# Adding the output bias of an attention block to the constant bin of its spectrum instead of to the whole of x

## The reference

```python
q = (layernorm(x) @ Wq + bq);  k = (ctx @ Wk + bk);  v = (ctx @ Wv + bv)   # k, v zero-padded to 2048 rows
qf, kf = rfft(q over rows), rfft(k over rows)
corr = irfft(qf.real * kf.real - 1j * qf.imag * kf.imag)
w, delay = top_k(mean of corr over heads and channels, 15);  w = softmax(w)
agg[t] = sum_i w[i] * v[(t + delay[i]) % 2048]
x = x + agg @ Wo + bo                                   # bo is the bias of this case
y = quantize_a16(layernorm(x))
h = quantize_a16(gelu(y @ quantize_w8(W_in) + b_in))
x = x + h @ quantize_w8(W_out) + b_out
```

## Time and profile before

| | us |
|---|---|
| median of 3 executions | 202.53 |
| lowest, highest | 200.09, 204.61 |
| the profiled execution's own time | 202.04 |
| its span, first to last instruction | 200.2 |

### The profile page before, as it was taken

The page is one execution under the profiler, slowest core; times in us unless marked ns, Lnnn a source line. Parts: engine busy times, 40 slices in busy tenths (PEclk is TensorE's granted clock), DMA queues, the critical chain, the costliest instruction groups (busy, mean ns, idle before and its releaser), DMA issues.

```text
span 200.2 us, 2844 instructions
## 1 busy us (share of the span) xinstructions
PE 172.7 (86%) x1051; PEld 127.5 (64%) x1054; DVE 153.5 (77%) x337; ACT 108.4 (54%) x172; POOL 31.8 (16%) x27
## 2 busy tenths in 40 slices
PE   8498999999129998989989974779999997999992
PEld 6398996447108976668985553754444455888881
DVE  0007977999998588789625799939998679999974
ACT  2225677533100264103464571789988858999930
POOL 8000000005950000000000005000592000532000
PEclk9859999999965899999999999589999999999999
DMA  3799994000000000000000000000000000001215
GB/s 109 217 290 402 411 357 158 0 5 0 0 0 0 0 3 0 2 0 0 0 3 0 0 3 0 0 0 0 5 0 0 0 0 3 0 0 56 105 52 210
DMA packets 6036, 11.96 MB, mean 60 GB/s; under 512 B 531, under 2 KB 3732, under 8 KB 5896
## 3 DMA queue, kind: packets, MB, share of 16 engines
q1 hardware_dynamic: 6024, 11.80, 17.0%
HBM read 9.70 MB, written 2.10 MB: 59 GB/s over the span
## 4 chain that ended last, share of the span: by engine, by line
PE 57%; DVE 24%; DMA 6%; ACT 5%; issue 3%; SPq 3%; DVEq 0%
PE ps L1171 12%; PE ps L1146 7%; PE ps L1141 6%; DMA arena<-wkT_dram 6%; PE ps L946 5%; DVE sm L651 4%; PE ps L965 4%; PE ps L1082 4%; DVE arena L633 3%; PE ps L997 3%; PE ps L1096 3%; PE ps L1005 2%; PE ps L1071 2%; PE ps L1121 2%; PE ps L1091 2%
## 5 line engine op out<-in xcount | busy, mean ns | idle before, releaser
L1171 PE MATMUL ps<-woutq,arena 128*128 128x256 f16 x256 | 28.7, 273 | 1.3 <-ACT arena L562 0.7
L1171 PEld LDWEIGHTS ps<-woutq,arena 128*128 128x128 f16 x256 | 24.7, 98 | 5.3 <-ACT arena L562 1.5
L547 ACT ACTIVATE arena<-ps,colv,sm 128x512 f32<-128x512 f32 x32 | 23.7, 781 | 2.1 <-PE ps L1146 0.5
L868 DVE SCALAR_TENSOR_TENSOR arena<-scr,sm,arena 128x1024 f16<-128x1024 int16 x16 | 21.3, 1372 | 0.0
L847 DVE TENSOR_REDUCE sm<-arena 128x1 f32<-128x1024 f32 (+1 forms) x17 | 18.9, 1148 | 2.5 <-ACT arena L547 2.5
L1146 PE MATMUL ps<-arena,winq 128*128 128x512 bf16 x64 | 18.6, 379 | 0.1
L1141 PE MATMUL ps<-arena,winq 128*128 128x512 bf16 x61 | 17.9, 379 | 0.7 <-ACT arena L539 0.7
L562 ACT ACTIVATE arena<-arena,sm 128x1024 f16<-128x1024 f32 x15 | 16.4, 1133 | 0.0
L946 PE MATMUL ps<-wvo,arena 128*128 128x256 f32 x64 | 15.4, 386 | 0.0
L901 PE MATMUL ps<-ones 128*128 128x256 bf16 x90 | 13.7, 311 | 1.0 <-POOL ones L349 1.0
L980 PE MATMUL ps<-arena,wqk 128*128 128x512 f32 x32 | 14.0, 594 | 0.1
(11 more groups left out here) (217 smaller groups left out, 332.3 us busy)
## 6 DMA issues: line engine op xcount, KB each, us to landing
tabs<-tab_dram SPq DMA_DIRECT2D x1, 2424.0 KB, 15.7
arena<-x_dram SPq DMA_DIRECT2D x4, 512.0 KB, 12.5
out_dram<-arena SPq DMA_DIRECT2D x8, 256.0 KB, 2.1
arena<-ctx_in_dram SPq DMA_DIRECT2D x3, 400.0 KB
arena<-winT_dram SPq DMA_DIRECT2D x1, 1024.0 KB, 17.0
arena<-wout_dram SPq DMA_DIRECT2D x1, 1024.0 KB, 19.2
arena<-ctx_in_dram SPq DMA_DIRECT2D x2, 200.0 KB
arena<-wqT_dram SPq DMA_DIRECT2D x1, 256.0 KB, 9.7
```

The source lines that it names most:

```text
L547: a.activation(H[:, f, 512 * c:512 * c + 512], bank("M1", n), ACT.Gelu, bias=colv[:, 6 + f:7 + f], scale=sc1[:, f:f + 1]).then_inc(S["h_re ...
L868: v.scalar_tensor_tensor(out=part, in0=scr16[:, n % 4, :], scalar=rf[:, f:f + 1], in1=piece(Hhi, n), op0=ALU.mult, op1=ALU.subtract).then_ ...
L1171: return t.matmul(o[k // 2][:, 256 * (k % 2):256 * (k % 2) + 256], part[:, t0:t0 + 128], woutq[:, f, :], start=start, stop=stop)
```

## The change

`bo` is no longer added to `xs` by GpSimd. It comes as two more columns of `colv` (14 for half 0 and 15 for half 1, one number a partition) and is added to the constant bin of each of the 16 groups b, 128 x 16 numbers of `cx` for each half: by ScalarE behind its copy of unit 0, by VectorE behind its copy of unit 1. Each of the two waits for its own copy first (`z_a`, `z_d`), and it, not the copy, raises `os_a` or `os_d`. `rowv` holds only b_out. The semaphore `xb_ready` and VectorE's wait for it go, and GpSimd's wait for the load of `rowv` moves to just ahead of the add of b_out.

```diff
-        colv = sb("colv", [128, 14])
-        rowv = sb("rowv", [128, 2 * D])
+        colv = sb("colv", [128, 16])
+        rowv = sb("rowv", [128, D])
...
-            sp.dma_start(rowv[:], rows[0:1, :].to_broadcast([128, 2 * D])).then_inc(S["ld_row"], 16)
+            sp.dma_start(rowv[:], rows[0:1, :].to_broadcast([128, D])).then_inc(S["ld_row"], 16)
...
             g.memset(BUT, 0.0).then_inc(S["bt_zero"], 1)
             pool.wait_ge(S["bt_zero"], 1)
-            pool.wait_ge(S["ld_row"], 16)
-            pool.wait_ge(S["xh_a"], 2)
-            pool.wait_ge(S["xh_d"], 2)
             x3 = xs.rearrange("p (b d) -> p b d", b=NB)
-            g.tensor_tensor(x3, x3, rowv[:, 0:D].unsqueeze(1).to_broadcast([128, NB, D]), ALU.add).then_inc(S["xb_ready"], 1)
-            pool.wait_ge(S["xb_ready"], 1)
...
+            pool.wait_ge(S["ld_row"], 16)
             pool.wait_ge(S["yq_ready"], 4)
-            g.tensor_tensor(x3, x3, rowv[:, D:2 * D].unsqueeze(1).to_broadcast([128, NB, D]), ALU.add).then_inc(S["x2b_ready"], 1)
+            g.tensor_tensor(x3, x3, rowv[:].unsqueeze(1).to_broadcast([128, NB, D]), ALU.add).then_inc(S["x2b_ready"], 1)
...
+        def constant_bin(h):
+            return cx[:, h * 2048:(h + 1) * 2048:128]
...
-                a.copy(spectrum(0, i // 2), bank("OO", i).rearrange("p (s b r) -> p b s r", b=NB, r=2)).then_inc(S["os_a"], 1)
+                ins_ = a.copy(spectrum(0, i // 2), bank("OO", i).rearrange("p (s b r) -> p b s r", b=NB, r=2))
+                if i == 0:
+                    ins_.then_inc(S["z_a"], 1)
+                    act.wait_ge(S["z_a"], 1)
+                    ins_ = a.activation(constant_bin(0), constant_bin(0), ACT.Identity, bias=colv[:, 14:15])
+                ins_.then_inc(S["os_a"], 1)
...
-                v.tensor_copy(spectrum(1, i // 2), bank("OO", i).rearrange("p (s b r) -> p b s r", b=NB, r=2)).then_inc(S["os_d"], 1)
-            dve.wait_ge(S["xb_ready"], 1)
+                ins_ = v.tensor_copy(spectrum(1, i // 2), bank("OO", i).rearrange("p (s b r) -> p b s r", b=NB, r=2))
+                if i == 1:
+                    ins_.then_inc(S["z_d"], 1)
+                    dve.wait_ge(S["z_d"], 1)
+                    ins_ = v.tensor_scalar(constant_bin(1), constant_bin(1), colv[:, 15:16], None, ALU.add)
+                ins_.then_inc(S["os_d"], 1)
```

More of the change, by code:

```diff
@@ L197, in build @@
         names = ("ld_F ld_wqk ld_tab ld_wv ld_win ld_wout ld_col ld_row "
-                 "pe dve_link act_link pool_const bu_ready xb_ready bt_zero x2b_ready nz_ready "
+                 "pe dve_link act_link pool_const bu_ready z_a z_d bt_zero x2b_ready nz_ready "
                  "xh_a xh_d qt_ready wqk_ready qc_ready bkb_ready qb_ready ownq_ready qbs_ready wvo_ready bvo_ready bvb_ready gram_a gram_d ab_ready own_ready "
@@ L1219 @@
         "wo": L0_xattn_Wo, "winT": np.asarray(L0_ffn_W_in).T, "wout": L0_ffn_W_out,
-        "cols": np.concatenate([cols(L0_xattn_bk), cols(L0_xattn_bq), cols(L0_xattn_bv), cols(L0_ffn_b_in)], 1),
-        "rows": np.concatenate([np.asarray(L0_xattn_bo), np.asarray(L0_ffn_b_out)])[None],
+        "cols": np.concatenate([cols(L0_xattn_bk), cols(L0_xattn_bq), cols(L0_xattn_bv), cols(L0_ffn_b_in), cols(L0_xattn_bo)], 1),
+        "rows": np.asarray(L0_ffn_b_out)[None],
         "tab": tab,
```

## The result

The changed kernel took 192.47 us (median of four executions, 191.75 to 192.84) against 203.42 us; the ratio is 0.9556, 95% interval 0.9446 to 0.9667. The ratios leave out executions more than 1.5% above the fastest of their kernel (two of the kernel before in the first measurement, 204.30 and 204.61 us), which the medians include. By the two ratios it is 4.4% and 5.5% faster. The forecast was 191.5 us, between 188.8 and 194.6.

A forecast was written before the change was run, and what follows sets the result against it. GpSimd's add of the output bias was taken to hold VectorE's L651, idling TensorE 8.04 us on the path. Stall -8.19, clock and waits -2.53, new additions 0: -10.7 us, giving 191.5 us, range 188.8 to 194.6.

The forecast's parts named there:

- L651 is held by GpSimd's add, and that is on the path: VectorE's L651 takes 8.36 us beside GpSimd's add, idling TensorE 8.04 us; without the add, L593 starts 8.19 us earlier.
- my other suspect: Rival: the add does not cause the stall, perhaps GpSimd's memset L364 just before it does; no gain, 202 us, chance 0.04.
- that step's heading: The step "The 8.9 us add on GpSimd goes": L651 falls to 0.17 us and L593 starts at 50.13, not 58.32.
- TensorE keeps its clock, worth 2.53 us: Gramian stretch: without the pause TensorE stays at 2.4 GHz, and VectorE's waits at L672, 1.80 and 0.73 us, go.
- everything behind L683 keeps its distance from it: After VectorE's L683, ending 10.72 us earlier at 63.04, all work from the 64x512 product L1033 on moves with it.
- only the direct stall comes back: Rival: the clock falls in 51 to 61 anyway or VectorE waits at L672; 2.53 us stay, 193.8 us; chance 0.12.
- what I had named to look for behind the stretch: Signs: next copies 10.7 us earlier, near 86.8 and 87.7; L1121 groups at about 106.3 and 115.5.
- The later dip: Rival: the low clock in 124 to 126, at L1121, moves; 1.5 us less (chance 0.11) or more (0.10).
- The two additions cost nothing: Constant bin: ScalarE's 0.3 us and VectorE's 0.23 us fit in idle time before the next copies, 1.10 and 0.55 us.
- The sum: Whole kernel: -8.19 - 2.53 + 0 = -10.7 us; this forecast's chance was 0.62.
- the two terms: Gramian stretch: 8.19 us for the direct stall and 2.53 us for TensorE's clock and VectorE's waits at L672.
- The forecast stretch of 15.92 us: First gramian to the 64x512 product: 15.92 us by the forecast's steps, against 26.64 us before.

The follow-up runs named there:

- e1: The changed kernel with GpSimd's add put back in its old place, its result written to unused xh and thrown away; 201.24 us, ratio 0.9902 to the kernel before.
- e5: The changed kernel, unaltered, run again beside other experiments; 191.45 us.
- e4: The changed kernel without the two additions to the constant bin, so the output lacks bo; 191.07 us, ratio 0.9498.
- e6: The changed kernel with 16 transposes of the quantised W_in moved ahead of the last second step, into TensorE's wait; 191.29 us, ratio 0.9459 to the kernel before.
- e7: The changed kernel with eight unneeded 128x256 bf16 products filling TensorE's pause ahead of the last second step; 191.09 us, ratio 0.9458.
- e2: The changed kernel with a GpSimd memset of 128x4096 in an unused place where the old add stood; 195.45 us, ratio 0.9692.
- e3: The kernel before, with GpSimd's add of bo cut into eight instructions of 128x512; 199.51 us, ratio 0.9893.

## Why the prediction was right, step by step

**L651 is held by GpSimd's add, and that is on the path.** Right, and shown by e1: the stall follows the GpSimd instruction and not its data. The memset L364, my other suspect, still runs in the changed kernel just ahead (1.81 us from 47.15), and L655 takes 0.17 us. I forecast L593 8.19 us earlier; it came at 50.23 for 58.32, that is 8.09, and 8.20 against the first gramian, which was 0.11 us late. (The 8.9 us of that step's heading is the other add's; this one took 8.81, and the sum doesn't use it.)

**TensorE keeps its clock, worth 2.53 us.** The two waits at L672 went, and from 54 to 59 the clock was 1.00. I had said 54 to 67; in 59 to 61 it was 0.78 and in 61 to 63 0.50. VectorE's L687 ended at 63.37 for a forecast of 63.04; 0.11 of the difference is the start, 0.19 a wait for TensorE's last second step. What failed is the sentence that everything behind L683 keeps its distance from it, TensorE included. I had found that TensorE would then wait for VectorE ahead of the last second step, but took that for harmless. In the profiled execution the clock fell there and cost 1.56 us by the difference of two executions of the same kernel. My rival "only the direct stall comes back" named this (the clock falls in 51 to 61 anyway) at 2.5 us; its mechanism came true in part, beside the forecast's. So what I had named to look for behind the stretch came late: the next copies at 88.52 and 89.42 for about 86.8 and 87.7, the two groups of transposes at 108.03 and 117.27 for 106.3 and 115.5. The 1.7 us had been lost by the 64x512 product (64.84 for 63.10).

**The later dip.** I had it as a rival at 1.5 us either way. It gave 0.80 us back in the profile and 1.00 in e5. Over all profiles from the 64x512 product to the first feed-forward product took 59.3 to 60.5 us.

**The two additions cost nothing.** Right: 0.32 and 0.25 us for a forecast of 0.3 and 0.23, without a table load, and the idle time shrank by about that. e4 shows the path unchanged to 0.01 us.

**The sum.** -10.7 us was forecast; the profiled executions differ by 9.8, 9.7 of them in the span: +0.1 from the loads, -9.1 in the stretch, -0.8 at the later dip. The medians differ by 10.95 and 11.02 us, and the two ratios stand for some 9.0 and 11.2 us. The mechanism and the two terms are shown; that the medians came within some 0.3 us of 10.7 is in part luck, since the end of the loads and the two dips move single executions by 1 to 2 us. The forecast stretch of 15.92 us stands beside 15.99, 15.98, 15.98 and 15.97 us in the four profiles without the dip (e5, e6, e7, e4).

## What to carry to other kernels

Work on GpSimd whose result nobody is waiting for can still hold up VectorE: look for tiny VectorE instructions with long rows, and see which GpSimd instruction ends with them. Count what such a stall costs twice, once as the time itself and once as TensorE's clock behind the pause, and then look for the wait that the new order creates on the other engine. A duration from one execution contains what the clock happened to do in it; comparing distances between the same two instructions separates them from the effect of an edit.

## What the runs showed of the hardware that I had not expected

- A GpSimd memset, which reads nothing, held a 128x8 `tensor_scalar` on VectorE for 3.03 us (e2), just as an add did for 8.36.
- A reciprocal on the same 128x8 operand in SBUF was not held (0.19 us within the add in pieces, e3), while the `tensor_scalar` on either side of it was (0.82 and 0.88).
- The GpSimd add cut in eight took 1.2 us more (10.03 for 8.81; whether by the cutting or by VectorE no run separates), and left six of VectorE's instructions at 0.8 to 1.25 us and a seventh at 0.60: smaller pieces made the loss smaller, they didn't remove it.
- The same kernel with the same wait on TensorE (1.00 and 0.99 us) kept 2.4 GHz in one execution and fell to 1.2 GHz in another, for 1.56 us of difference.
